# A place of its own for each prologue step on every engine, and two small VectorE operations that read one operand from PSUM

## The chip, the cores and the metric

The kernel runs on one core of one Trainium2 chip. TensorE (PE), VectorE (DVE), ScalarE (ACT), GpSimd (POOL) and SyncE (SP, which only issues DMAs here) each run their own instruction stream in order and meet through semaphores. The metric is the device time in microseconds of one execution.

## What is computed

Eight images (B = 8, 128 channels, 16 x 16 = 256 tokens) go through two residual layers:

```
x = x + L0(groupnorm(x))     # linear attention with rope, a 5x5 depthwise conv of v ("lepe"), a gate o, a projection
x = x + L1(groupnorm(x))     # layernorm, 4 channel groups through a Mamba block, layernorm, a projection

# inside the Mamba block, per channel group and token t (16 states per channel):
delta = softplus(dt @ W_dt.T + b_dt);  A = -exp(A_log)
h = exp(delta_t * A) * h + (delta_t * u_t) * B_t      # a scan over the 256 tokens
y_t = sum over states of h * C_t, then + u_t * D, then * silu(z)
```

## The kernel before

All work is in fp32. The batch index b is the image. The work of an image is split into **chains** of steps, one generator per chain and engine; a step is the code between two `yield`s.

- `front(b)`: normalise, the q, k, v, o products, softmax, rope, and the 128x128 matrix KVM (DVE line 989). In order: xg0, qk, QK and kraw, vo, vpad (its copy goes through DRAM to V4), oS, eff, nmx, exp, rE, kk (line 984, "QK<-F,rE,kraw"), Mk, den, tq and tk on POOL (835, 837), rope, QR and lz, zS, kvT, KVT, kv, KVM.
- `lepe(b)`: eight rounds of conv matmuls on PE (line 404), which need V4 in SBUF.
- `mid(b)`: res on PE, u1 and u2 on DVE (998, 1002), u3 on POOL, proj on PE, sums on ACT, g2 on PE, then ga, nv, ms on DVE (1006, 1009, 1014) with lnv and rs on ACT between nv and ms, xg, xc, sq, var, lr, rr, xl (DVE 1018), XN (ACT 697). XN goes through DRAM (`xn_out`, line 235) and comes back as XN4 in four shifted copies (line 239).
- `tail(b)`: Mamba's inputs. xp, z, dt on PE, the silus, the softplus pieces ab, em, um1, lnu on ACT (714 to 724), cor on DVE (1025), dl1, delta, du on POOL (851 to 858), bc on PE and ACT. bc goes through DRAM and comes back broadcast as Bs and Cs (line 257); delta goes out in the `spill` (246) and comes back broadcast in `load_delta` (265).
- `lead(0)`: the same for image 0 alone; here DVE does dl1 to du (1034 to 1044) and delta is broadcast by PE (line 490, `delta_bc`) instead of through DRAM.
- `weights`: products of weights, and the statistics of images 1 to 7.
- `back(b)`: y2 on DVE (1052), output projection, second layernorm (xl2, 1055), store.

The scan itself is no chain: each image has eight **units** g = 0 to 7. On DVE a unit is one multiply into BIN (line 1082, in PSUM, by Bs) and one scan (line 1107, needs `decay` of ACT, line 789); on POOL it is one multiply by Cs (line 882, `hc`), on PE one `collect` (557), one unit behind. A unit has four slots (segments) in which `side()` runs the steps of other images' chains whose number has come. On DVE two slots lie between multiply and scan and two behind the scan; on POOL two lie ahead of its multiply and two behind.

So the order on each engine is fixed by numbers alone. A **period** of 32 segments holds the eight units of image b and beside them back(b-1), tail(b+1), mid(b+2), front(b+3) and lepe(b+3): the `yield`s are their segments, and on every engine a step with a lower number goes first. What runs ahead of period 1 is a **prologue**: `PROLOGUE` gives each chain of images 0 to 3 an offset and a rate (`at + number * rate // 8`), the same on all engines; START is the segment where image 0's units begin; whatever has a number beyond START + 32 runs behind the units and ahead of period 1. These numbers order instructions on an engine, nothing more: between engines only semaphores count.

```
            for g in range(GROUPS):
                seg = iter(range(START + SIDES * g, START + SIDES * (g + 1)))
                unit(0, 0, g, lambda: segment(works, next(seg)), True)
            run(works, START + SEGMENTS, 7 * SEGMENTS)
            with eng.Fori(0, (B - 4) // 2) as pair:
                period(2 * pair + 1, 1)
                period(2 * pair + 2, 0)
```

The last two images (6, 7) have their units cut in halves (lines 1078, 1094, 1097).

## Time and profile before

| | |
|---|---|
| runs shown | 387.08, 385.05, 385.3 us; median 385.3 |
| profiled execution | 385.47 us, of which the span from the first to the last instruction is 383.7 us |
| mean granted TensorE clock in the span | 0.860 |
| busy, share of span | PE 279.8 us (73%), DVE 282.9 (74%), ACT 221.0 (58%), POOL 201.1 (52%) |
| first multiply of image 0's units | 86.79 us |
| first multiply of period 1 | 128.69 us |
| first multiply of period 6 (half units) | 314.35 us |

Times are microseconds from the span's start. The share of busy time is a mean over stages: ahead of 86.8 us DVE is nearly idle, between 128 and 375 us it is the engine that is busiest.

### The profile page before, as it was taken

How to read it: one execution, taken by the hardware profiler on the slowest of the kernel's cores; microseconds unless marked ns; L12 is line 12 of the kernel's file. 1: busy time of each engine (PE TensorE's matmuls, PEld its weight loads, DVE VectorE, ACT ScalarE, POOL GpSimd, SP SyncE). 2: the span in 40 equal slices, each digit the busy share in tenths (PEclk: the TensorE clock that was granted, in tenths of full speed). 3: DMA queues.
4: the chain of work that ended last, by engine and by line, in shares of the span. 5: the costliest groups of instructions: out<-in, count | busy, mean ns of one | idle time of the engine just before them, and what ended most of it. 6: DMA issues, size and time to landing. Idle time of an engine off the chain costs nothing.

```text
span 383.7 us, 5569 instructions
## 1 busy us (share of the span) xinstructions
PE 279.8 (73%) x1882; PEld 133.0 (35%) x1882; DVE 282.9 (74%) x342; ACT 221.0 (58%) x408; POOL 201.1 (52%) x135
## 2 busy tenths in 40 slices
PE   2398697389849687978796859877986756856764
PEld 1164334153315333433343325334532422312221
DVE  1622242109887699988997799889999989899992
ACT  2324574546845686669765866687657538634211
POOL 0020100014676368746864658458748757967760
PEclk9999699558967988999899878997999669678588
DMA  7230308750048915791589057915890397177000
GB/s 268 73 78 25 86 15 288 290 118 2 30 121 261 331 49 129 262 335 58 126 274 346 33 126 249 332 71 127 277 340 15 93 289 290 41 284 276 2 0 27
DMA packets 27075, 61.73 MB, mean 161 GB/s; under 512 B 2992, under 2 KB 14896, under 8 KB 27056
## 3 DMA queue, kind: packets, MB, share of 16 engines
q1 hardware_dynamic: 26768, 60.88, 49.6%
q10 hardware_dynamic: 288, 0.61, 0.4%
q8 instruction: 11, 0.18, 0.2%
q14 instruction: 8, 0.07, 0.1%
HBM read 54.62 MB, written 6.86 MB: 160 GB/s over the span
## 4 chain that ended last, share of the span: by engine, by line
PE 40%; DVE 21%; ACT 16%; issue 11%; DMA 9%; POOL 1%; SPq 1%; ACTq 0%; DVEq 0%; POOLq 0%
DVE hst L1107 7%; PE F L404 6%; PE DB L530 4%; DMA delta_scratch<-delta 4%; DVE DB L1082 4%; DMA dlt<-delta_scratch 3%; PE Y L557 3%; PE F L382 3%; DVE hst L1094 2%; DVE DB L1078 2%; PE F L373 2%; DVE hst L1097 2%; PE F L352 2%; PE F L390 2%; DMA CCs<-cc 1%
## 5 line engine op out<-in xcount | busy, mean ns | idle before, releaser
L882 POOL TENSOR_TENSOR hst<-hst,Cs 128x1024 f32<-128x1024 f32 x48 | 113.2, 2359 | 62.0 <-DVE hst L1107 62.0
L1107 DVE TENSOR_TENSOR_SCAN hst<-dec,DB 128x1024 f32<-128x1024 f32 x48 | 109.6, 2283 | 1.3
L789 ACT ACTIVATE dec<-dlt,negA 128x1020 f32<-128x1020 f32 x60 | 68.3, 1145 | 21.1 <-DMA dlt<-delta_scratch 14.6
L1082 DVE TENSOR_TENSOR DB<-DB,Bs 128x1024 f32<-128x1024 f32 x48 | 58.9, 1226 | 2.7 <-PE DB L530 1.7
L557 PE MATMUL Y<-hst,CCs 128*32 128x256 f32 x512 | 47.9, 431 | 10.0 <-POOL hst L879 5.4
L879 POOL TENSOR_TENSOR hst<-hst,Cs 128x512 f32<-128x512 f32 x31 | 38.7, 1269 | 15.2 <-DVE hst L1094 15.2
L404 PE MATMUL F<-V,wpatch 128*32 128x256 f32 x512 | 38.4, 419 | 0.9 <-DVE xl L1018 0.9
L846 POOL TENSOR_TENSOR u<-u,oS 128x256 f32<-128x256 f32 x8 | 5.8, 729 | 51.0 <-DVE u L1002 51.0
L835 POOL TENSOR_TENSOR tq<-QK,W0s 128x512 f32<-128x512 f32 x8 | 8.7, 1091 | 42.8 <-DVE QK L984 42.8
L530 PE MATMUL DB<-du,CCs 32*128 32x512 f32 x64 | 22.8, 793 | 8.8 <-DVE DB L1078 5.5
L557 PEld LDWEIGHTS Y<-hst,CCs 128*32 128x32 f32 x512 | 14.9, 117 | 37.0 <-issue 18.1
L404 PEld LDWEIGHTS F<-V,wpatch 128*32 128x32 f32 x512 | 15.2, 117 | 19.1 <-issue 12.9
L989 DVE TENSOR_TENSOR KVM<-F,CCs 128x128 f32<-128x128 f32 x8 | 2.3, 292 | 26.4 <-PE F L390 26.4
L429 PE MATMUL F<-xg,CCs 128*128 128x256 f32 x16 | 8.3, 613 | 17.9 <-ACT xg L682 17.9
L1078 DVE TENSOR_TENSOR DB<-DB,Bs 128x512 f32<-128x512 f32 x32 | 20.5, 687 | 0.6 <-PE DB L530 0.4
L1094 DVE TENSOR_TENSOR_SCAN hst<-dec,DB 128x512 f32<-128x512 f32 x16 | 19.3, 1209 | 0.0
L1097 DVE TENSOR_TENSOR_SCAN hst<-dec,DB 128x512 f32<-128x512 f32 x16 | 19.1, 1194 | 0.0
L773 ACT ACTIVATE X<-F,bout 128x256 f32 (+1 forms) x7 | 3.3, 475 | 26.2 <-PE F L520 26.2
L453 PE MATMUL F<-XN,W1s 128*32 128x256 f32 x112 | 8.4, 421 | 10.9 <-ACT xs L704 10.9
L352 PE MATMUL F<-xg,W0s 128*128 128x256 f32 x32 | 9.8, 434 | 5.0 <-ACT xg L617 4.1
L461 PE MATMUL F<-xs,W1s 128*64 128x512 f32 x14 | 8.2, 668 | 6.9 <-DVE cor L1025 6.9
L622 ACT ACTIVATE r_qk<-F,W0s 128x256 f32<-128x256 f32 x16 | 6.7, 471 | 11.0 <-PE F L352 11.0
(176 smaller groups left out, 538.8 us busy)
## 6 DMA issues: line engine op xcount, KB each, us to landing
Bs<-bc_scratch SPq DMA_DIRECT2D x32, 512.0 KB, 6.5
Cs<-bc_scratch SPq DMA_DIRECT2D x32, 512.0 KB, 7.3
dlt<-delta_scratch SPq DMA_DIRECT2D x15, 512.0 KB, 4.7
V<-v_scratch SPq DMA_DIRECT2D x32, 200.0 KB, 3.7
XN<-xn_scratch SPq DMA_DIRECT2D x28, 128.0 KB, 3.3
delta_scratch<-delta SPq DMA_DIRECT2D x16, 128.0 KB, 4.4
v_scratch<-vpad SPq DMA_DIRECT2D x8, 211.5 KB, 2.1
bc_scratch<-bc SPq DMA_DIRECT2D x8, 128.0 KB
```

The source lines that it names most:

```text
L352: last = mm(F0[:, T * i:T * i + T], wt("wqkvo", C * i, C), xg0[:], start=True, stop=True)
L404: last = mm(F1[CM * q:CM * q + CM, 0:T], wpatch[:, ROUNDS * q + n, :], img[:, :, 0:W], start=(n == 0), stop=(n == ROUNDS - 1))
L530: last = mm(DU[:, half, :], wt("pick")[p0:p0 + DD], du[j][p0:p0 + DD, :], start=True, stop=True)
L557: last = mm(Y[CM * i:CM * i + CM, T * kg:T * kg + T], wt("place"), hst[g % 4][:, T * i:T * i + T], start=False, stop=(g % 4 == 3))
L789: af(dec[g % 4][:, :, 1:T], dlt[2 * j + g // SG][:, :, 1:T], ACT.Exp, scale=negA[:, g:g + 1]).then_inc(S("decay_ready"), 1)
L879: tt(part, part, halves(Cs[g % SG], half), ALU.mult).then_inc(S(signal), 1)
L882: tt(hst[g % 4][:], hst[g % 4][:], Cs[g % SG][:], ALU.mult).then_inc(S("hc_ready"), 1)
L1078: v.tensor_tensor(BIN[:, half, :], DU[:, half, :], halves(Bs[g % SG], half), ALU.mult).then_inc(S(signal), 1)
L1082: v.tensor_tensor(flat(BIN), flat(DU), Bs[g % SG][:], ALU.mult).then_inc(S("b_ready"), 1)
L1094: v.tensor_tensor_scan(halves(hst[g % 4], 0), flat(dec[g % 4][:, 0:2, :]), BIN[:, 0, :], 0.0, ALU.mult, ALU.add).then_inc(S("h_half"), 1)
L1097: v.tensor_tensor_scan(halves(hst[g % 4], 1), flat(dec[g % 4][:, 2:4, :]), BIN[:, 1, :], 0.0, ALU.mult, ALU.add).then_inc(S("h_ready"), 1)
L1107: v.tensor_tensor_scan(hst[g % 4][:], flat(dec[g % 4][:]), flat(BIN), 0.0, ALU.mult, ALU.add).then_inc(S("h_ready"), 1)
```

## The change

Four things, in one diff.

1. `PROLOGUE` goes. Each engine gets a table `places` with one number for each step of each chain, and `segment` takes the step with the lowest number first. START is 100. In the new order image 0's chains come first, then image 1's; the units of image 0 begin on DVE behind lead(0), front(1), u1 and u2 of mid(1) and QK and kraw of front(2).
2. What stood ahead of START and no longer does goes into the 32 segments of image 0's units or, above 132, behind them and ahead of period 1. On DVE ga(2), nv(2), ms(2), cor(1), nmx(3), xl(2), rE(3), kk(3), KVM(3) stand behind the units.
3. The `yield` numbers of the periods 1 to 7 change on all engines. On DVE: u1, u2 and QK 7, 7, 4 to 5, 6, 6; y2 3 to 2; nv and ms from 14 to 15 and 16 (ga stays at 14); nmx 16 to 15; kk 21 to 17; xl2 27 to 24; KVM 31 to 26. On PE: qk 2 to 0, xp 3 to 2, kvT and kv 27 and 29 to 22 and 23, the conv rounds 24 to 30 become 20 to 31. On ACT: lr2 and rr2 27 to 25, KVT 29 to 25, QR and lz 27 to 22, XN 19 to 24, bc 15 to 11. On POOL: u3 2 to 8, delta 13 to 11, tq and tk 19 and 21 to 14. The SP numbers are in the diff.
4. nv and ms read the group mean from F1 in PSUM in place of its copy ga in SBUF.

```diff
-        def begin(chain, b, j, at=0, rate=8):
-
-            steps = chain(b, j)
-            return [steps, at + next(steps, IDLE) * rate // 8, at, rate]
+        def advance(work):
+
+            step = next(work[0], IDLE)
+            work[1] = step if work[2] is None else next(work[2], IDLE)
+
+        def begin(chain, b, j, places=None):
+
+            work = [chain(b, j), 0, None if places is None else iter(places)]
+            advance(work)
+            return work
 
         def segment(works, s):
 
-            for work in works:
-                while work[1] == s:
-                    work[1] = work[2] + next(work[0], IDLE) * work[3] // 8
-
-        def periods(eng, chains, start, unit, finish):
+            while works:
+                work = min(works, key=lambda candidate: candidate[1])
+                if work[1] > s + 1 - 1e-6:
+                    return
+                advance(work)
+
+        def periods(eng, chains, places, start, unit, finish):
 
 
...
-            works = [begin(chain, k, k % 2, *at) for chain, k0, starts in zip(
-                (tail, lead, mid, lepe, front, weights), (1, 0, 0, 0, 0, 0), PROLOGUE) for k, at in enumerate(starts, k0)]
+            works = [begin(chain, k, k % 2, steps) for chain in (tail, lead, mid, lepe, front, weights)
+                     for k, steps in places.get(chain.__name__, {}).items()]
...
-        PROLOGUE = (((130, 9),), ((78, 6),), ((61, 6), (96, 6), (134, 6)), ((16, 12), (61, 7), (88, 13), (122, 9)), ((30, 7), (53, 11), (100, 5), (128, 10)), ((36, 5),))
-        START = 127
+        START = 100
...
             def front(b, j):
 
-                yield 5
+                yield 6
                 sp.wait_ge(S("vpad_ready"), b + 1)
                 sp.dma_start(v_dram, vpad[:]).then_inc(S("v_out"), 16)
-                yield 9
+                yield 17
                 sp.wait_ge(S("v_out"), 16 * (b + 1))
...
             def mid(b, j):
 
-                yield 15
+                yield 21
                 if isinstance(b, int) and b == 0:
                     return
                 sp.wait_ge(S("xn_ready"), b + 1)
                 sp.dma_start(xn_dram, XN[j][:]).then_inc(S("xn_out"), 16)
-                yield 25
+                yield 22
...
             def tail(b, j):
 
-                yield 10
+                yield 17
                 sp.wait_ge(S("bc_ready"), b + 1)
                 sp.dma_start(bc_dram[j].rearrange("w s (h n) -> h (w s) n", h=2), bc[:]).then_inc(S("bc_out"), 16)
-                yield 12
+                yield 17
                 spill(b, j)
-                yield 12
+                yield 18
                 load_delta(b, j, 0)
                 load_delta(b, j, 1)
...
+            places = {
+                "tail": {
+                    1: (96.882, 104.059, 111.235,),
+                },
+                "lead": {
+                    0: (39.471, 46.647,),
+                },
+                "mid": {
+                    0: (3.588,),
+                    1: (68.176, 75.353,),
+                    2: (118.412, 124,),
+                },
+                "front": {
+                    0: (10.765, 17.941,),
+                    1: (25.118, 32.294,),
+                    2: (53.824, 61,),
+                    3: (82.529, 89.706,),
+                },
+            }
+            periods(sp, (weights, front, lepe, mid, tail, back, lead), places, lambda: None, unit, lambda: None)
...
             def lepe(b, j):
 
                 for n, (dy, dx) in enumerate(PLACES):
-                    yield (24, 25, 26, 26, 27, 28, 29, 30)[n]
+                    yield (20, 20, 23, 24, 28, 31, 31, 31)[n]
...
             def tail(b, j):
 
-                yield 3
+                yield 2
                 pe.wait_ge(S("xn_shifted"), 16 * DCONV * b)
...
+                "tail": {
+                    1: (122.6, 125, 127.333, 128.222,),
+                },
+                "lead": {
+                    0: (67.073, 71.951, 100.7,),
+                },
...
+                    1: (98.78, 103.5, 104.9, 111.5, 114.5,),
+                    2: (121.8, 127.111, 127.778, 128, 128.444,),
+                },
...
+                    2: (116.429, 117, 117.571, 118.143, 118.714, 119.4, 120.2, 121,),
+                    3: (128.889, 129.111, 129.333, 129.556, 130, 130.222, 130.444, 146.25,),
...
+                    2: (86.585, 102.1, 106.3, 109, 112.5, 113.5, 115.286,),
+                    3: (115.857, 127.556, 128.667, 129.778, 130.667, 130.889, 176.75,),
+                },
...
-                yield 27
+                yield 22
                 act.wait_ge(S("rope_done"), b + 1)
...
-                yield 29
+                yield 25
                 act.wait_ge(S("kvT_done"), b + 1)
                 nc.scalar.copy(flat(KVT[:]), F0[:]).then_inc(S("kvT_ready"), 1)
...
+                yield 19
                 act.wait_ge(S("xc_done"), b + 1)
...
-                yield 19
+                yield 24
                 act.wait_ge(S("xl_ready"), b + 1)
...
-                yield 6
+                yield 9
                 wait(act, "dl1_ready", b)
                 af(lnu[:], F2[:], ACT.Ln, bias=1.0).then_inc(S("lnu_ready"), 1)
-                yield 15
+                yield 11
                 act.wait_ge(S("bc_done"), b + 1)
                 wait(act, "bc_out", 16 * b)
                 nc.scalar.copy(bc[:], F2[0:2 * 2 * DS, :]).then_inc(S("bc_ready"), 1)
...
+                "tail": {
+                    1: (122.095, 122.476, 123.048, 123.238, 123.81, 124.381, 124.571,),
+                },
+                "lead": {
+                    0: (87.5, 95.833, 104.091,),
+                },
...
+                    1: (105, 107.727, 108.636, 109.545, 114.25, 115.25, 116.25, 116.75,),
+                    2: (122.286, 122.857, 123.429, 123.619, 124.19, 124.952, 125.333, 125.714,),
...
+                    1: (37.5, 40.278, 45.833, 48.611, 51.389, 56.944, 65.278, 70.833, 81.944, 84.722, 90.278,),
+                    2: (93.056, 98.611, 100.455, 101.364, 102.273, 103.182, 105.909, 106.818, 111, 113, 114.75,),
+                    3: (115.75, 117.25, 117.75, 122.667, 124, 124.762, 125.143, 125.524, 125.905, 145.5, 176.5,),
...
+            places = {
+                "tail": {
+                    1: (124, 125.333,),
+                },
+                "mid": {
+                    0: (42.5,),
+                    1: (93.5,),
+                    2: (122.667,),
+                },
+                "front": {
+                    0: (8.5, 25.5,),
+                    1: (59.5, 76.5,),
+                    2: (107, 109,),
+                    3: (145.5, 176.5,),
+                },
+            }
+            periods(pool, (weights, front, lepe, mid, tail, back, lead), places, lambda: None, unit, lambda: None)
...
-                yield 14
+                yield 15
                 dve.wait_ge(S("ga_ready"), b + 1)
-                v.scalar_tensor_tensor(out=nv[:], in0=ga[:, 0:1], scalar=ga[:, 0:1], in1=ga[:, 1:2],
+                v.scalar_tensor_tensor(out=nv[:], in0=F1[:, 0:1], scalar=ga[:, 0:1], in1=ga[:, 1:2],
                                        op0=ALU.mult, op1=ALU.subtract).then_inc(S("nv_ready"), 1)
-                yield 14
+                yield 16
                 dve.wait_ge(S("rs_ready"), b + 1)
                 wait(dve, "xg_ready", b)
-                v.scalar_tensor_tensor(out=ms[:], in0=ga[:, 0:1], scalar=-1.0, in1=rs[:],
+                v.scalar_tensor_tensor(out=ms[:], in0=F1[:, 0:1], scalar=-1.0, in1=rs[:],
                                        op0=ALU.mult, op1=ALU.mult).then_inc(S("ms_ready"), 1)
...
+            places = {
+                "tail": {
+                    1: (154.111,),
+                },
+                "lead": {
+                    0: (79.032, 85.484,),
+                },
+                "mid": {
+                    0: (40.323, 43.548, 56.452, 59.677, 62.903, 75.806,),
+                    1: (88.71, 98.387, 109.167, 109.5, 109.833, 117.5,),
+                    2: (126.333, 127.667, 133.444, 140.333, 147.222, 167.889,),
+                },
+                "front": {
+                    0: (1.613, 4.839, 14.516, 20.968, 24.194, 37.097,),
+                    1: (46.774, 53.226, 66.129, 69.355, 72.581, 82.258,),
+                    2: (91.935, 95.161, 108.167, 108.5, 108.833, 116.5,),
+                    3: (119, 127, 161, 174.778, 181.667, 188.556,),
+                },
+                "weights": {
+                    0: (8.065, 11.29, 17.742, 27.419, 30.645, 33.871, 50,),
+                },
+            }
+            periods(dve, (weights, front, lepe, mid, tail, back, lead), places, lambda: None, unit, lambda: None)
```

## Rows read from the trace of the kernel before

**Rows 1.** Groups of DVE instructions 128.7 to 312 us, shapes apart: xcount, busy, mean ns, idle before

```profile
L1014 DVE SCALAR_TENSOR_TENSOR ms<-ga,rs 128x1 f32<-128x1 f32 x5 | 4.9, 983 | 3.0 <-ACT rs L678 3.0
L1025 DVE SCALAR_TENSOR_TENSOR cor<-um,F 128x512 f32<-128x512 f32 x5 | 3.4, 688 | 2.9 <-ACT lnu L724 2.8
L1052 DVE TENSOR_TENSOR y<-Y,zs 128x512 f32<-128x512 f32 x5 | 3.4, 681 | 2.3 <-PE Y L557 2.3
L1009 DVE SCALAR_TENSOR_TENSOR nv<-ga 128x1 f32<-128x1 f32 x5 | 2.9, 581 | 0.2
...
L1055 DVE SCALAR_TENSOR_TENSOR xl<-F,W1s,rr 128x256 f32<-128x256 f32 x5 | 2.4, 484 | 2.7 <-ACT rr L767 2.7
...
L998 DVE TENSOR_TENSOR u<-F,zS 128x256 f32<-128x256 f32 x5 | 2.1, 419 | 1.3 <-PE F L414 1.3
...
L989 DVE TENSOR_TENSOR KVM<-F,CCs 128x128 f32<-128x128 f32 x4 | 1.2, 292 | 3.6 <-PE F L390 3.6
L1006 DVE COPY ga<-F 128x2 f32<-128x2 f32 x5 | 0.7, 133 | 0.0
```

**Rows 2.** The timeline on DVE: start, us, instruction, idle before it and its releaser

```profile
86.79 1.23 DVE L1082 TENSOR_TENSOR DB<-DB,Bs 128x1024 f32<-128x1024 f32 x1 [1.73 <-PE DB L530]
...
120.73 2.29 DVE L1107 TENSOR_TENSOR_SCAN hst<-dec,DB 128x1024 f32<-128x1024 f32 x1
...
128.69 1.23 DVE L1082 TENSOR_TENSOR DB<-DB,Bs 128x1024 f32<-128x1024 f32 x1
...
314.35 1.30 DVE L1078 TENSOR_TENSOR DB<-DB,Bs 128x512 f32<-128x512 f32 x2
```

**Rows 3.** Three source lines over the whole span: duration in ns, min/median/max

```profile
L1009 DVE SCALAR_TENSOR_TENSOR nv<-ga x8: 219/424/1311, 38.8 to 296.1; 128x1 f32<-128x1 f32 x8
...
L1014 DVE SCALAR_TENSOR_TENSOR ms<-ga,rs x8: 159/784/1700, 39.7 to 297.5; 128x1 f32<-128x1 f32 x8
...
L1018 DVE SCALAR_TENSOR_TENSOR xl<-F,W1s,rr x8: 460/475/483, 44.0 to 302.9; 128x256 f32<-128x256 f32 x8
```

**Rows 4.** The timeline around lead(0), all engines

```profile
51.79 0.69 ACT L748 ACTIVATE ab<-F,W1s 128x512 f32<-128x512 f32 x1
...
52.85 0.67 SPq L283 DMA_DIRECT2D bc_scratch<-bc  x1
...
55.96 0.69 DVE L1044 TENSOR_TENSOR du<-delta,xs 128x512 f32<-128x512 f32 x1
...
58.09 0.58 SPq L257 DMA_DIRECT2D Bs<-bc_scratch  x1
```

**Rows 5.** The timeline on POOL in image 0's units

```profile
105.56 1.25 POOL L851 TENSOR_TENSOR dl<-lnu,cor 128x512 f32<-128x512 f32 x1
...
120.69 2.37 POOL L882 TENSOR_TENSOR hst<-hst,Cs 128x1024 f32<-128x1024 f32 x1
123.02 1.09 POOL L837 TENSOR_TENSOR tk<-QK,W0s 128x512 f32<-128x512 f32 x1
```

**Rows 6.** The chain that ended last: start, us, what

```profile
148.51 5.25 DMA delta_scratch<-delta
153.78 4.02 DMA dlt<-delta_scratch
157.88 1.15 ACT dec L789
```

**Rows 7.** The timeline on ACT in period 3

```profile
216.53 0.60 ACT L717 ACTIVATE F<-ab 128x512 f32<-128x512 f32 x1
```

**Rows 8.** The timeline on the DMA queue of SP, end of period 1, and DVE in period 2

```profile
155.13 0.51 SPq L235 DMA_DIRECT2D xn_scratch<-XN  x1
...
160.56 1.73 SPq L239 DMA_DIRECT2D XN<-xn_scratch  x4
162.41 0.52 SPq L257 DMA_DIRECT2D Bs<-bc_scratch  x1
...
169.84 1.22 DVE L1082 TENSOR_TENSOR DB<-DB,Bs 128x1024 f32<-128x1024 f32 x1
```

More of the change, by code:

```diff
@@ L284, in lead @@
                 load_bc(b, j, 0)
-                yield 16
+                yield 26
                 spill(b, j)
@@ L309, in weights @@
                 yield from ()
-            periods(sp, (weights, front, lepe, mid, tail, back, lead), lambda: None, unit, lambda: None)
+            places = {
[18 more added lines that the diff above has]
+            periods(sp, (weights, front, lepe, mid, tail, back, lead), places, lambda: None, unit, lambda: None)
             sp.wait_ge(S("stored"), 16 * B)
@@ L816, in _ @@
             setup()
-            periods(act, (weights, front, lepe, mid, tail, back, lead), start, unit, lambda: None)
+            places = {
[6 more added lines that the diff above has]
+                "mid": {
[3 rows of a table added]
+                },
+                "front": {
[4 rows of a table added]
+                },
+                "weights": {
+                    0: (20.833, 26.389,),
+                },
+            }
+            periods(act, (weights, front, lepe, mid, tail, back, lead), places, start, unit, lambda: None)
         @block.gpsimd
```

160 lines of the change are left out of this document (87 added, 73 removed), and 6 rows, old and new, of the table places.

## The prediction

> **What bounds the kernel now.** I read the waits of DVE, then the groups of its instructions, then its timeline unit by unit, then the chain that ended last and the DMA queue. Between the first multiply of period 1 (128.69) and that of period 6 (314.35) lie five periods in 185.7 us, 37.1 each [rows 2]. In them DVE works or waits for small things: ms for rs 3.0 us, cor for lnu 2.9, y2 for the last collect 2.3, xl2 for rr2 2.7, u1 for res 1.3, KVM for kv 3.6, together 15.8 us [rows 1]. A second loss is hidden in busy time. nv and ms are one element wide; their shortest cases take 0.219 and 0.159 us, but nv goes up to 1.311 and ms to 1.700, while xl, the same kind of instruction with 256 elements and one tensor from PSUM, stays within 0.460 to 0.483 [rows 3]. In the five periods their means are 0.581 and 0.983, so the excess is 5 x (0.581 - 0.219) + 5 x (0.983 - 0.159) = 5.9 us [rows 1, 3]. Both have SBUF operands only, and POOL is in its long multiply then. Without waits and excess the five periods would be 185.7 - 15.8 - 5.9 = 164.0 us, 32.8 each. So DVE sets the periods, and there is up to 21.7 us to win.
>
> Ahead of period 1 it is otherwise: dependent chains set the time. The units of image 0 begin at 86.79, though du(0), which they need, is done at 56.65 [rows 4]; front(2) and mid(1) stand between. The units end with the scan at 120.73 to 123.02, and 5.7 us of gap follow until 128.69 [rows 2].
>
> **The change, part by part.**
>
> *First multiply of image 0.* I wrote out the new order of each engine and followed it. The start of the profile is the same up to QK and kraw of image 0, and XN(0) comes about 1 us sooner, since mid(0) no longer waits behind front(1). Against it, on ACT ab of lead(0) stands behind KVT(1) and xg0(2): ab moves from 51.79 to about 53.6, and du(0) ends near 58.4 instead of 56.65. Behind du DVE has u1, QK, kraw, u2, until 60.5. Bs(0) is issued at the end of the bc round trip, 58.09 - 52.85 = 5.2 us behind its write [rows 4], so at about 57.2, and lands near 61. First multiply 61; the decays need delta_bc and come at 62.3. The first scan ends near 64.9 instead of 90.3: 25.4 us sooner. Work that stood ahead of it is not gone; it is owed below.
>
> *Image 0's units.* Old: 86.79 to 123.02, 36.2 us [rows 2]. New: 8 units at 3.6 us (multiply 1.23, scan 2.29) are 28.8; beside them stand nmx, rE, kk, ga, nv, ms, KVM, xl, QK, u1, kraw, u2, together 4.1 us; waits inside are 2.0 in unit 2 (eff, exp, lnv and rs in a row) and 1.1 for KVM(2). Sum 36.0, last scan at 97.5; I allow 1 us for what I can't see: 98.5.
>
> *The gap.* Here the debt is paid. ACT takes lnv(2) ahead of em, um1, lnu of tail(1), and DVE reaches ga, nv, ms(2) and then cor(1) only behind the last scan. From the last scan to the end of cor: ga 0.13, nv 0.22, lnv and rs 0.6, ms 0.16, then em, um1, xg, lnu at 0.60 [rows 7], cor 0.69 [rows 1], 4.2 us, with hand-offs and the wait for g2(2) 5.9: 104.4. Then POOL, which has dl1, delta, du *ahead of* its multiplies 6 and 7, and tq, tk(3) behind them: 3 x 1.25 + 2 x 2.37 + 2 x 1.09 + hand-offs 0.4 = 11.1 [rows 5]: 115.5. From tk to the next multiply the old trace takes 128.69 - 124.11 = 4.6 us (kvT, KVT, kv, KVM) [rows 2, 5]; in the new order two decays of 1.15 [rows 6] stand on ACT ahead of KVT: 6.9. First multiply of period 1: 122.4. The other branch, delta through DRAM, ends about there too: delta done at 107, spill 5.25, load 4.02, decay 1.15 [rows 6], 117.4. So the gap is 24 us instead of 5.7, and what remains of the 25 us is 128.7 - 122.4 = **6.3 us**. Bounds: each engine's list may hide waits in the gap (least saving 0, the gap 6 us longer); if all my allowances fall away, 9.
>
> *nv and ms from PSUM.* They become what xl is, one tensor from PSUM, and xl never shows the excess [rows 3]. A PSUM source costs nothing that the rows show: ga copies two elements out of PSUM in 0.133 [rows 1]. **5.9 us** in periods 1 to 5 (bounds 0 and 5.9). The Trainium skill speaks against it: "VectorE: DVE Perf Modes", section on the TRN2 errata, gives a fixed 120 cycles for a PSUM source and 58 for SBUF, an estimate of 65 ns for each of 16 instructions, 1.0 us in all; the 0.133 us of ga is no longer than an SBUF instruction of that width, and the trace decides. For the cause the skill ("SBUF — State Buffer", section "Who interferes with whom") has a lock on a read port between POOL and a DVE instruction with two SBUF inputs, held for a whole instruction; the longest case of 1.7 us against POOL's 2.37 fits it.
>
> *The new order in the periods.* nv at 14 or 15 and ms at 16 put nmx and a multiply between them, which hides lnv and rs: 3.0 us. KVM at 26 needs kk at 17: about 10.5 us of DVE work between them, while the chain kk to KVM needs about 9; besides, QR, lr2, rr2 and KVT of ACT now precede the decay that waits for load_delta. So KVM's 3.6 goes, and of xl2's 2.7 most. lnu comes sooner as qk no longer waits for a KVM at 31: of cor's 2.9, 2 go. u1's 1.3 goes. y2's 2.3 stays: xp stands ahead of that collect now. Sum of waits removed 3.0 + 3.6 + 2.0 + 2.0 + 1.3 = 11.9.
> What is late next: the round trip of XN. XN goes at 24 on ACT, behind a decay, QR, lz, zS; xn_out to XN4 took 160.56 - 155.13 = 5.4 us, XN4's four issues 1.8, and only then is Bs of the next image's unit 1 issued (162.41), 7.4 us ahead of its multiply (169.84) [rows 8]. With shorter periods those 7.4 us shrink by about 1.5 to 2 and some of the load shows: I charge 1.0 us a period, 4.8 in all. Net 11.9 - 4.8 = **7.1** (bounds 3.0, the part that is plain, and 13).
>
> *Periods 6 and 7* have no nv, ms or front; one wait for lnu goes: 0.5.
>
> Sum: 6.3 + 5.9 + 7.1 + 0.5 = 19.8. The profiled execution has 385.5 us, 0.2 above the median of 385.3. 385.5 - 19.8 = 365.7; **366 us**.
>
> **Rivals.**
> *The gap eats the prologue's gain.* The gap chain runs over five engines, and every number in it is a least case. If period 1 starts at 128.7 as now: 385.5 - 13.5 = 372. For it: 24 us of pure dependence. Against it: the sum has slack in the eff and DMA branches.
> *The PSUM operand doesn't do it.* The excess stays, if its cause is another: 366 + 6 = 372. Against it: [rows 3].
> *The order gives its gain back.* Only rs's 3.0 us come from it: 370.
> *Slower: XN's round trip becomes the bound.* Each period would be as long as XN to XN4 to Bs. To lose against now, a period must pass 37.1 + 6.3 / 5 = 38.4, from 32.8: XN must be late by 5.6 us more than the slack, where place 24 instead of 19 explains 2 to 3. At 1.5 us beyond that point: 393. For it: Bs waits in the same queue behind XN4 [rows 8]. Against: SP's spill is now ahead of V4's load, so the loads of delta clear sooner.
>
> **How the numbers follow.** Main case 0.57, own range 358 to 370; gap 0.14; order given back 0.10; PSUM 0.06; XN bound 0.07; the rest 0.06 spread near no change. A measurement here can tell about 0.5% from no change. The range leaves out 0.2: from 357, all allowances falling away, to 378, two of the losses together. Faster 0.87, same 0.05, slower 0.08.
>
> **What would show it.** Right: first multiply near 61, last scan of image 0 near 98, period 1 from 122; a hole in DVE of some 24 us between them with POOL busy in it; nv and ms at 0.2 us in all eight images; no wait at KVM; five periods in some 173 us. Wrong: Bs or XN4 as releaser of DVE or PE in each period; a first multiply of period 1 behind 128; nv or ms still at 0.8.

## The result and the profile after

The changed kernel takes 374.5 us (median of 4 runs, 373.62 to 378.18) against 385.6 (4 runs, 385.05 to 387.08). The ratio is 0.9755, 95% interval 0.971 to 0.980: faster by 11.1 us by the medians, by 9.4 us (7.7 to 11.2) by the ratio. The forecast was 19.8 us and a time of 366. The sign is right and the time lies inside the whole range (357 to 378), but outside the main case's own range (358 to 370), and the gain is about half of the one predicted. In the profiled executions 385.47 becomes 374.03, and the span 383.7 becomes 372.2: 11.5 us to be placed.

(Some executions of a kernel are more than 1.5% longer than its fastest: below, medians and ranges are over all executions, ratios and their intervals leave the longer ones out and decide where the two differ, and the profiled executions of three experiments, V4's load alone, no PSUM operands and the gap, are such longer ones, so that their rows show which wait stands where and not what it costs.)

The page of the kernel after, span and busy times of the engines:

```profile
span 372.2 us, 5571 instructions
PE 274.4 (74%) x1882; PEld 128.2 (34%) x1882; DVE 275.2 (74%) x342; ACT 220.1 (59%) x408; POOL 201.5 (54%) x135
```

Its timeline on DVE, the rows that answer to [rows 2], and the end of the prologue:

```profile
60.49 1.23 DVE L1174 TENSOR_TENSOR DB<-DB,Bs 128x1024 f32<-128x1024 f32 x1 [1.08 <-DMA Bs<-bc_scratch]
...
93.88 2.29 DVE L1199 TENSOR_TENSOR_SCAN hst<-dec,DB 128x1024 f32<-128x1024 f32 x1
...
121.01 0.29 DVE L1081 TENSOR_TENSOR KVM<-F,CCs 128x128 f32<-128x128 f32 x1 [13.76 <-PE F L416]
121.44 1.23 DVE L1174 TENSOR_TENSOR DB<-DB,Bs 128x1024 f32<-128x1024 f32 x1
...
302.40 1.30 DVE L1170 TENSOR_TENSOR DB<-DB,Bs 128x512 f32<-128x512 f32 x2
```

The 11.5 us split by these starts and [rows 2]. Up to the first multiply of period 1: 128.69 - 121.44 = 7.25 gained (forecast 6.3). Periods 1 to 5: 185.66 - 180.96 = 4.7 gained (forecast 13.0). The rest of the program: 69.35 before, 69.8 after, 0.45 lost (forecast 0.5 gained). So 8.3 us are missing in the periods and 1 more at the end, and the prologue gave 1 more than forecast.

By the first multiplies of image 0 of each period in the two timelines, periods 1 to 5 took 36.3, 37.7, 39.9, 37.3, 34.5 before and take 36.6, 37.6, 38.0, 37.5, 31.2 now. The first four take 149.7 us instead of 151.1. The fifth, in which no front and no conv are left, is shorter by 3.3 us, more than the 2.6 a period that the forecast came to. So of the 4.7 us only 1.4 come from the four periods in which all chains run.

The groups of DVE instructions of the kernel after in 123 to 305 us (count, busy us, mean ns, idle us before and what ended it), beside [rows 1]:

```profile
L1144 DVE TENSOR_TENSOR y<-Y,zs 128x512 f32<-128x512 f32 x5 | 3.4, 681 | 2.2 <-PE Y L583 2.2
L1117 DVE SCALAR_TENSOR_TENSOR cor<-um,F 128x512 f32<-128x512 f32 x5 | 3.4, 677 | 1.2 <-ACT lnu L778 1.2
L1147 DVE SCALAR_TENSOR_TENSOR xl<-F,W1s,rr 128x256 f32<-128x256 f32 x5 | 2.4, 482 | 13.4 <-ACT rr L821 13.4
L1090 DVE TENSOR_TENSOR u<-F,zS 128x256 f32<-128x256 f32 x5 | 2.1, 415 | 0.0
L1081 DVE TENSOR_TENSOR KVM<-F,CCs 128x128 f32<-128x128 f32 x4 | 1.1, 278 | 0.2
L1101 DVE SCALAR_TENSOR_TENSOR nv<-F,ga 128x1 f32<-128x1 f32 x5 | 1.1, 219 | 0.2
L1106 DVE SCALAR_TENSOR_TENSOR ms<-F,rs 128x1 f32<-128x1 f32 x5 | 0.7, 149 | 0.0
```

Row by row the forecast held: ms no longer waits for rs (3.0 to 0.0), KVM fell from 3.6 to 0.2, u1 from 1.3 to 0.0, cor from 2.9 to 1.2, and nv and ms run in 219 and 149 ns. One row stands against it: xl2 (line 1147) waits 13.4 us for rr2 where it waited 2.7. Most of what the other waits lost stands at this one place now.

What keeps rr2 is read on the other engines, in the time before the DVE wait. Period 2 of the kernel after, the timeline on the DMA queue of SP:

```profile
173.12 0.36 SPq L225 DMA_DIRECT2D v_scratch<-vpad  x1
174.95 0.56 SPq L279 DMA_DIRECT2D bc_scratch<-bc  x1
176.29 1.14 SPq L253 DMA_DIRECT2D delta_scratch<-delta  x2
177.55 3.16 SPq L229 DMA_DIRECT2D V<-v_scratch  x4
```

on PE and ACT, and the wait on DVE, in the same period:

```profile
181.75 1.03 PE L399 MATMUL F<-tq,CCs 128*128 128x256 f32 x4
...
185.19 1.19 PE L430 MATMUL F<-V,wpatch 128*32 128x256 f32 x16 [2.41 <-DMA V<-v_scratch]
186.31 1.22 PE L540 MATMUL F<-sq,CCs 128*128 128x256 f32 x2
...
187.57 0.47 ACT L818 ACTIVATE lr<-F,CCs 128x256 f32<-128x256 f32 x1 [3.16 <-PE F L540]
188.07 0.42 ACT L821 ACTIVATE rr<-lr 128x256 f32<-128x256 f32 x1
...
188.53 0.48 DVE L1147 SCALAR_TENSOR_TENSOR xl<-F,W1s,rr 128x256 f32<-128x256 f32 x1 [2.85 <-ACT rr L821]
```

Read it upwards. DVE waits 2.85 us for rr2. rr2 and lr2 of ACT wait 3.16 us for the matmul of the variance (line 540). That matmul needed its square at 180.5 (ACT's sq2 ran there), but on PE it stands behind two conv rounds (line 430), which wait 2.41 us for V4. V4's load starts at 177.55, though its own input v_out was written from 173.12 on: on SP it now stands behind the bc write and the spill of delta. The waits of PE over all periods of the kernel after (us in total, times, longest) say that it is so each time:

```profile
PE F L430 <- DMA V<-v_scratch: 10.6, 4, 2.9
```

Two ends moved against each other. V4's load went from place 9 to 17 on SP: it is issued 19.5 us after the period's first multiply (177.55 - 158.08), before at 181.93 - 164.95 = 17.0. The first conv rounds went from places 24 and 25 on PE to 20: they are ready to run some 25 us into the period, before at 194.32 - 164.95 = 29.4. So the first conv round came 12.4 us behind the issue of the load; now PE is ready for it some 5 us behind, and V4 lands 7.6 us behind (185.19 - 177.55).

### The profile page after: what moved, and what is told of

Same layout as the page of the kernel before. It is cut to its first block, busy times and chain, and to the rows that moved or that the text cites. A ratio compares the mean times of both kernels' runs of the same rounds, so it can differ in the third digit from the quotient of the medians.

```text
span 372.2 us, 5571 instructions
## 1 busy us (share of the span) xinstructions
PE 274.4 (74%) x1882; PEld 128.2 (34%) x1882; DVE 275.2 (74%) x342; ACT 220.1 (59%) x408; POOL 201.5 (54%) x135
## 4 chain that ended last, share of the span: by engine, by line
PE 26%; DVE 17%; issue 17%; DMA 12%; ACT 12%; POOL 10%; SPq 4%; POOLq 1%; DVEq 0%; ACTq 0%
POOL hst L958 6%; DVE hst L1199 4%; DMA V<-v_scratch 4%; PE F L430 4%; PE Y L583 3%; DVE DB L1174 3%; DVE hst L1186 2%; PE DB L556 2%; DMA Cs<-bc_scratch 2%; DVE DB L1170 2%; SPq L229 2%; PE F L378 2%; PE F L408 2%; DMA CCs<-cc 1%; POOL delta L931 1%
## 5 line engine op out<-in xcount | busy, mean ns | idle before, releaser
L583 PE MATMUL Y<-hst,CCs 128*32 128x256 f32 x512 | 50.1, 429 | 11.7 <-POOL hst L955 9.5
L430 PE MATMUL F<-V,wpatch 128*32 128x256 f32 x512 | 38.2, 423 | 12.6 <-DMA V<-v_scratch 10.6
L556 PE MATMUL DB<-du,CCs 32*128 32x512 f32 x64 | 21.2, 742 | 4.4 <-DVE DB L1170 3.3
L1147 DVE SCALAR_TENSOR_TENSOR xl<-F,W1s,rr 128x256 f32<-128x256 f32 x8 | 3.8, 480 | 16.4 <-ACT rr L821 16.4
L676 ACT ACTIVATE r_qk<-F,W0s 128x256 f32<-128x256 f32 x16 | 6.7, 470 | 14.4 <-PE F L378 14.4
L408 PE MATMUL F<-CCs,tk 128*128 128x128 f32 x64 | 13.7, 356 | 0.8 <-ACT lz L708 0.8
L408 PEld LDWEIGHTS F<-CCs,tk 128*128 128x128 f32 x64 | 12.7, 267 | 4.3 <-ACT lz L708 2.0
L573 PE MATMUL Y<-xs,dsel 128*32 128x256 f32 x128 | 12.0, 452 | 2.2 <-DVE y L1144 2.0
```

Source lines behind the costliest of these rows:

```text
L408: mm(F0[:, P * blk:P * blk + P], tk[:, which, P * blk:P * blk + P], wt(turn), start=(which == 0), stop=(which == 1))
L430: last = mm(F1[CM * q:CM * q + CM, 0:T], wpatch[:, ROUNDS * q + n, :], img[:, :, 0:W], start=(n == 0), stop=(n == ROUNDS - 1))
L556: last = mm(DU[:, half, :], wt("pick")[p0:p0 + DD], du[j][p0:p0 + DD, :], start=True, stop=True)
L583: last = mm(Y[CM * i:CM * i + CM, T * kg:T * kg + T], wt("place"), hst[g % 4][:, T * i:T * i + T], start=False, stop=(g % 4 == 3))
```

## The experiments

Kernels of one job shared the chip and the runs of the kernel before: its median was 385.8 us (11 runs) for the first job, 385.6 (16) for the second, 384.9 (11) for the third. The executions of one kernel spread by 4 to 12 us, so differences of 2 us between two medians are not relied on. Where us are given "by the ratio", they are the ratio and its interval times the median of the kernel before.

### First job: is it V4's load, and what is PSUM worth?

**V4's load back in front of bc and spill**, on the changed kernel:

```
-                yield 17
+                yield 10
                 sp.wait_ge(S("v_out"), 16 * (b + 1))
```

> One number is changed against the changed kernel: SP issues V4's load at place 10 of a period, ahead of the writes of bc and delta, as before, in place of 17 behind them. Theory A (V4's load comes late because SP stands at the wait for delta; the first two conv rounds then hold PE, var2 behind them, lr2 and rr2 on ACT, xl2 on DVE): the wait of DVE at xl2, 13.4 us in periods 1 to 4, falls under 2 us, PE no longer waits for V4 (10.6 us now), and the time falls by 8 to 12 us, to 363 to 367. Rival B (xl2 is late because ACT has lr2 and rr2 behind QR, lz, zS and XN at places 22 and 24): the wait at xl2 stays above 2 us in each period and the time stays within 2 us of 374.5. Rival C (another engine takes over): xl2's wait goes, but waits for PE or for Bs take its place and the time falls by less than 5 us.

Measured: 371.6 us (368.14 to 375.09), ratio 0.957 [0.952, 0.963], by the ratio 16.6 us below the kernel before (14.4 to 18.7). The waits of DVE and of PE in this kernel, 120 to 302 us:

```profile
DVE y L1144 <- PE Y L583: 14.3, 4, 4.7
```

```profile
PE F L472 <- DMA XN<-xn_scratch: 11.7, 4, 4.0
```

The wait at xl2 is gone, so V4's load was its cause. But nearly the same 14 us now stand at y2, which waits for a collect matmul, which stands on PE behind xp (line 472), which waits for XN4. That is the first link of the rival named in the prediction, XN's round trip; in the changed kernel PE waits nothing for XN4. Against the change the net gain is 2.9 us by the medians and 7.1 by the ratios (4 to 10), and none in the profiled execution, of 374.4 us. That execution has one more loss, which none of the waits above names: its first four periods take 144.5 us against 149.7 in the changed kernel, its fifth 38.2 against 31.2, and in the fifth the granted clock of TensorE is 0.74 against 0.94. More on this at the third job.

**The other remedy: the variance's matmul ahead of the conv rounds**, V4 as late as in the change:

```
-                yield 22
+                yield 20
                 pe.wait_ge(S("sq2_ready"), b + 1)
```

> V4's load stays late, but var2 is issued on PE at place 20, ahead of the two conv rounds that wait for it (22 before). Theory A: the wait at xl2 goes almost wholly, as var2 no longer stands behind the wait for V4; but kvT, KVT and kv still do, so part comes back as a wait at KVM of about 2 us a period; the time falls by 3 to 7 us, to 367 to 371. Rival B: nothing changes, 374.5 within 2.

Measured: 370.3 us (368.61 to 373.83), ratio 0.961 [0.956, 0.966], 15.1 us by the ratio, 4 to 6 below the change. DVE's waits, 120 to 310 us:

```profile
DVE KVM L1081 <- PE F L416: 9.7, 4, 3.4
```

xl2's wait is gone here too, which shows the link through PE's order. V4 is still late (PE waits 8.7 us for it), and what now stands behind the conv rounds is the kv matmul.

**The PSUM operands alone**, on the kernel before: `in0=ga[:, 0:1]` becomes `in0=F1[:, 0:1]` in nv and ms.

> The kernel before with nv and ms reading the mean from F1 in PSUM and nothing else. Theory A (a VectorE instruction of two SBUF tensors waits for GpSimd's running multiply, and DVE sets the periods): nv and ms fall to 0.22 and 0.16 us in all images and the time falls by 5 to 7.6 us, to 378 to 380.5. Rival: the short instructions are cured but the time is given back at the next wait (KVM, cor): under 2 us gained.

Measured: 382.5 us (378.76 to 384.7), ratio 0.985 [0.979, 0.990]: 3.3 us by the medians, 6.0 by the ratio (3.7 to 8.2). Durations of the two lines (min/median/max ns):

```profile
L1009 DVE SCALAR_TENSOR_TENSOR nv<-F,ga x8: 219/219/220, 39.0 to 293.2; 128x1 f32<-128x1 f32 x8
```

```profile
L1014 DVE SCALAR_TENSOR_TENSOR ms<-F,rs x8: 157/158/159, 39.8 to 294.0; 128x1 f32<-128x1 f32 x8
```

The excess goes entirely, as forecast. Whether the time follows entirely isn't decided: the interval of the ratio holds the 5.9 us forecast, while the one profiled execution is only 2.4 us shorter. In it the five periods take 184.2 us instead of 185.7 (period 1 starts 2.1 sooner), and xl2's wait is 6.4 us instead of 2.7, so in this execution most of what the periods should have won came back there.

**The change without the PSUM operands**: the same edit the other way round.

> The changed kernel with nv and ms reading SBUF again. Theory A: their durations go up again to a mean of 0.6 and 0.9 us in periods 1 to 5. Since DVE waits 3.4 us at xl2 behind them in each of periods 1 to 4 in any case, most of that is swallowed by that wait: the time rises by less than 3 us over 374.5. Rival: the whole 5.9 us come back, 380.

Measured: 374.7 us (369.0 to 377.93), ratio 0.963 [0.956, 0.970]: no loss; by the ratio it is even the faster of the two, in another job. nv goes up to 1079 ns and ms to 2347, 10.0 us more in the five periods than in the changed kernel, but xl2's wait is 4.9 instead of 13.4 us, and the five periods take 181.7 us against 181.0. In the kernel as changed no gain of the PSUM operand can be measured: most of what DVE saves by it, it waits at xl2.

### Second job: down the list of limits, and the parts

**xp behind the collect**: the first experiment, and on PE xp at place 3 instead of 2.

```
-                yield 2
+                yield 3
                 pe.wait_ge(S("xn_shifted"), 16 * DCONV * b)
```

> V4's load at 10 and, beside it, xp of the next image at place 3 on PE (behind the last collect, as before) in place of 2 (ahead of it). The run with V4's load early alone moved the wait of DVE from xl2 to y2 (14.7 us in five periods), because PE stood at xp for XN4 with the last collect behind it. Theory A2 (XN's round trip through DRAM is what is late, and it costs only through the collect behind xp): y2's wait falls under 3 us, the time falls by 7 to 11 us against the run with V4 early alone, to 361 to 365. Rival (xp itself is then late, and with it silu, dt, lnu and cor): DVE waits at cor for 2 us and more a period instead, the time stays near 370.

Measured: 369.4 us (365.85 to 371.3), ratio 0.960 [0.954, 0.966], by the ratios no gain over the first experiment; expected were 7 to 11 us. The waits of DVE, 120 to 302 us:

```profile
DVE DB L1174 <- DMA Bs<-bc_scratch: 9.1, 7, 1.8
```

y2's wait is gone as expected, and its place is taken by Bs, which is issued in SP's queue behind XN4.

**XN's write ahead of delta's loads**: the first experiment, and on SP xn_out at 18 instead of 21, load_delta at 19 instead of 18.

> V4's load at 10 and, beside it, SP issues XN's write ahead of the loads of delta (18 and 19) in place of behind them (21 and 18); xp stays ahead of the collect. Theory A2: XN's write no longer queues behind 1 MB of delta, XN4 lands 2 to 4 us sooner, PE's wait at xp (11.7 us in four periods) falls to under 5 and y2's wait with it; the time falls by 4 to 8 us to 364 to 368. Rival (the round trip is bound by its own latency, or SP by XN being late): the wait at xp stays above 8 us.

Measured: 382.0 us (378.76 to 384.94, 12 runs), ratio 0.992 [0.988, 0.996]: 10 us slower than the first experiment by the medians, 13 by the ratios, where a gain was expected. The DMA issues of this kernel (count, KB each, median us from issue to landing):

```profile
Bs<-bc_scratch SPq DMA_DIRECT2D x32, 512.0 KB, 7.7
...
XN<-xn_scratch SPq DMA_DIRECT2D x28, 128.0 KB, 7.2
...
xn_scratch<-XN SPq DMA_DIRECT2D x7, 129.5 KB, 2.3
```

and of the first experiment:

```profile
Bs<-bc_scratch SPq DMA_DIRECT2D x32, 512.0 KB, 6.2
...
XN<-xn_scratch SPq DMA_DIRECT2D x28, 128.0 KB, 3.6
...
xn_scratch<-XN SPq DMA_DIRECT2D x7, 129.5 KB, 4.9
```

The write does land sooner, 2.3 us instead of 4.9. But delta's loads then run beside the XN4 loads instead of beside the write, and these take 7.2 us instead of 3.6. Bs and Cs of the next unit, 1 MB, come closer too: in period 2 delta, Bs and Cs, 2 MB in all, are issued in the 3.0 us ahead of XN4 here (184.42 to 187.42) and in the 7.0 us ahead of it in the first experiment (180.43 to 187.39). Which of the two slows XN4, no run told apart. PE's wait at xp is 16.6 us (from 11.7), y2's 18.2 (from 14.3). Write and loads together take 9.5 us instead of 8.5 by these medians, and Bs behind them 7.7 instead of 6.2.

**The prologue alone**: explicit places and START = 100, but the old yields inside the periods and SBUF operands.

```
-            works = [begin(chain, k, k % 2, *at) for chain, k0, starts in zip(
+            works = [begin(chain, k, k % 2, steps) for chain in (tail, lead, mid, lepe, front, weights)
...
-        START = 127
+        START = 100
```

> The new places of the prologue and START = 100, with the place numbers of the periods, and the SBUF operands of nv and ms, of the kernel before. Theory A: the first multiply of period 1 comes at 121 to 123 as in the changed kernel (128.7 before), and the rest takes the 255 us that it took before: 377 to 380. Rival (the periods' gain in the changed kernel hangs on both together): above 383 or below 375.

Measured: 377.4 us (374.57 to 383.69), ratio 0.979 [0.971, 0.986], 8.2 us by the medians; period 1 starts at 118.86, and the five periods take 184.2 us. This is most of what the whole change gives; the spans of the two profiled executions, 372.8 and 372.2 us, are nearly the same. With the old order in the periods, period 1 starts 2.6 us sooner than in the changed kernel.

**The gap of the changed kernel**: on PE den, rope and kvT of image 3 ahead of the conv rounds, on ACT zS and KVT ahead of the two decays.

```
-                    3: (128.889, 129.111, 129.333, 129.556, 130, 130.222, 130.444, 146.25,),
+                    3: (128.889, 129.3, 129.5, 150, 150.2, 150.4, 150.6, 150.8,),
...
-                    3: (115.857, 127.556, 128.667, 129.778, 130.667, 130.889, 176.75,),
+                    3: (115.857, 127.556, 128.667, 129.1, 129.2, 129.4, 145,),
...
-                    3: (115.75, 117.25, 117.75, 122.667, 124, 124.762, 125.143, 125.524, 125.905, 145.5, 176.5,),
+                    3: (115.75, 117.25, 117.75, 122.667, 124, 124.762, 125.143, 125.524, 125.905, 125.92, 125.94,),
```

> The changed kernel with another order in the gap ahead of period 1: on PE den, rope and kvT of image 3 stand ahead of conv rounds 1 to 7 (rounds 3 to 7 behind kv), and on ACT zS and KVT ahead of the first two decays of period 1. In the changed kernel tq is done at 110.0 but rope starts at 115.45, behind six conv rounds. Theory G (in the gap PE's order, not POOL's chain, ends last): the first multiply of period 1 comes 2 to 4 us sooner, at 117.5 to 119.5, part of which y2 or u2 gives back; the time falls by 1 to 3 us. Rival (POOL's chain or the loads of delta end last): no change at the first multiply.

Measured: 373.5 us (370.65 to 378.86), ratio 0.970 [0.964, 0.976]. Period 1 starts 3.9 us sooner, at 117.50, and then takes 39.7 us instead of 36.6. DVE's waits of this kernel in period 1, where the kernel after has only the one at xl2, 3.4 us:

```profile
DVE y L1144 <- PE Y L583: 3.1, 1, 3.1
DVE xl L1147 <- ACT rr L821: 2.8, 1, 2.8
```

The order in the gap did set the first multiply. What was won is paid back at y2, behind PE's wait of 1.9 us for XN4 at xp: the transfers did not come sooner with the units. (This is read from one execution, of 378.9 us; the last kernel of the third job gives its earlier start back too, at other rows.)

### Third job: the periods alone, and the last limit

**The new order in the periods alone**: old prologue, new yields, SBUF operands.

> The opposite half of the prologue run: the old order of the prologue, with the new place numbers of the periods, nv and ms from SBUF. Theory A (V4's late load at xl2 gives back what the new numbers win): periods 1 to 5 take 182 to 187 us (185.7 before) and the time stays within 2 us of 385.5. With the prologue alone at about -8 and the PSUM operand alone at about -3 the three parts then add up to the change's -11. Rival (the new numbers win by themselves and the prologue loses it): 380 or less.

Measured: 380.9 us (379.94 to 385.42), ratio 0.9925 [0.987, 0.998], 4.0 us by the medians, 2.9 by the ratio (0.7 to 5.0). The periods take 181.6 us; KVM, rs and u1 no longer wait inside them, xl2 waits 5.3. Between what the two theories expected: the order is worth something, and less than the 7.1 us forecast for it.

**Half of delta's load behind Bs**: the kernel with V4 early and xp at 3, and in `tail` on SP the second half of delta's load at place 30.

```
                 load_delta(b, j, 0)
+                yield 30
                 load_delta(b, j, 1)
...
-                    1: (96.882, 104.059, 111.235,),
+                    1: (96.882, 104.059, 111.235, 130,),
```

> V4's load at 10, xp at 3, and the load of delta's second half (0.5 MB, first needed by unit 4 of the next period) at place 30 in place of 18. With V4 early and xp behind the collect DVE waited for Bs 9.1 us. Theory D (what is left late is the DMA traffic in the second half of a period: 1 MB of delta, XN and 1 MB for each unit's Bs and Cs): the wait for Bs falls under 4 us and the time by 2 to 5 us, to 364 to 367. Rival (Bs is late because it is issued behind XN4 on SP, whatever is ahead in the queues): Bs waits stay above 7 us, the time stays at 369.

Measured: 363.9 us (360.25 to 365.88), ratio 0.942 [0.936, 0.947]: 21 us faster than before by the medians and 22 by the ratio, 11 to 13 faster than the change. DVE's waits, 120 to 302 us:

```profile
DVE DB L1175 <- DMA Bs<-bc_scratch: 3.6, 4, 1.1
DVE ga L1099 <- PE F L452: 2.1, 1, 2.1
DVE xl L1111 <- ACT rr L747: 1.4, 1, 1.4
DVE cor L1118 <- ACT lnu L779: 0.6, 2, 0.4
```

Bs's 9.1 us fell to 3.6, xp's wait on PE from 9.5 to 4.0, and periods 1 to 5, 119.65 to 289.14, take 169.5 us, 33.9 each. The prediction had computed 32.8 for a period without waits or excess. That Bs's wait fell under 4 us is what theory D expected and its rival did not. But two things left the way of XN and Bs at once: the traffic of half of delta, and 1.3 us of SP's time for issuing it (in period 2 delta's issues ahead of XN's write take 0.56 us instead of 1.87; from that write to XN4 it is then 4.15 us instead of 5.05). No run separates them.

The five periods are not alike. The first four take 33.3 us on average; the fifth, which has the least work in it, takes 36.2. The rows of the fifth period in the kernel after and in this one (start to end, its length, then busy time and count of PE, PEld, DVE, ACT and POOL; then the granted clock of TensorE, DMA share, GB/s):

```profile
271.17:302.40 31.23, 22.21 (x168) 8.47 (x160) 30.54 (x25) 22.66 (x35) 23.24 (x13) 0.94 0.53 180
```

```profile
252.92:289.14 36.22, 26.03 (x156) 10.19 (x152) 30.84 (x25) 21.80 (x36) 23.32 (x13) 0.77 0.60 199
```

DVE does the same work in both, and PE is busy 3.8 us longer, with fewer matmuls. From 266.9 to 274.9 us the granted clock of this kernel is 0.50, the lower of its two levels (1.2 GHz of 2.4), after 4 us (262.9 to 266.9) in which PE had been busy for 1.4. The same two groups of matmuls in the kernel after, at full clock, and here:

```profile
283.44 1.07 PE L487 MATMUL F<-xs,W1s 128*64 128x512 f32 x2 [0.54 <-DVE cor L1117]
...
285.01 1.13 PE L556 MATMUL DB<-du,CCs 32*128 32x512 f32 x4
```

```profile
266.74 1.97 PE L488 MATMUL F<-xs,W1s 128*64 128x512 f32 x2 [1.01 <-DVE cor L1118]
...
269.64 2.08 PE L557 MATMUL DB<-du,CCs 32*128 32x512 f32 x4
```

The matmul for ga stands behind these, which is the wait of 2.1 us at ga in the list above. In the other kernels with V4's load early and PSUM operands the fifth period is as slow: 38.2, 36.8, 37.7 and 38.3 us at 0.74, 0.78, 0.77 and 0.74. With V4 late and the variance's matmul moved instead it takes 31.9 us at 0.93. So they are 5 to 7 us longer than the changed kernel there; no run was made to take this back, or to show what brings the clock down.

**V4 early and xp at 3, with SBUF operands**, to price the PSUM operand where DVE sets the pace:

> V4's load at 10 and xp at 3, but nv and ms from SBUF. In the changed kernel the waits at xl2 swallowed their excess. Theory A says that here less is swallowed, as the xl2 wait is gone, but the Bs wait behind it still takes a part: the time rises by 2 to 5 us over 369.4. Rival: nothing, 369.4 within 1.5.

Measured: 376.6 us (369.54 to 381.89), ratio 0.964 [0.957, 0.972], against 369.4 and a ratio of 0.960 [0.954, 0.966] with PSUM operands in another job. The medians are 7 us apart, but the ratios only 1.8, which is well inside their intervals, and the profiled executions 3.4 (372.85 and 369.47), of which 3.1 us lie ahead of period 1. So neither the 2 to 5 us expected nor the rival, nothing, is ruled out. The two traces show both sides of it: with SBUF operands the first four periods take 145.3 us instead of 139.8, and the fifth, at a granted clock of 0.89 instead of 0.78, takes 32.5 instead of 36.8. Durations in this kernel:

```profile
L1101 DVE SCALAR_TENSOR_TENSOR nv<-ga x8: 219/1002/1302, 37.9 to 285.5; 128x1 f32<-128x1 f32 x8
```

```profile
L1106 DVE SCALAR_TENSOR_TENSOR ms<-ga,rs x8: 158/686/2341, 38.9 to 286.8; 128x1 f32<-128x1 f32 x8
```

**All together with another order in the gap**:

```
-                    3: (128.889, 129.111, 129.333, 129.556, 130, 130.222, 130.444, 146.25,),
+                    3: (128.889, 129.2, 129.3, 129.6, 129.65, 129.8, 150, 150.2,),
...
-                    3: (115.857, 127.556, 128.667, 129.778, 130.667, 130.889, 176.75,),
+                    3: (115.857, 127.556, 128.667, 129.1, 129.4, 129.7, 145,),
```

> V4's load at 10, xp at 3, delta's second half late, and in the gap ahead of period 1 den, rope and kvT of image 3 ahead of most conv rounds, rounds 1 to 5 in the pauses and 6 and 7 behind kv, KVT ahead of the first decays. Theory D and G together: the first multiply of period 1 comes at 116 to 118.5, two thirds of these 3 us are kept: 2 us less than without the gap's edit, 362 to 365. Rival (period 1 gives the gap's gain back whole, as its tail then waits for XN4 and Bs): the same time as without it.

Measured: 364.0 us (359.72 to 366.96), ratio 0.944 [0.938, 0.949], the same as without it. Period 1 starts at 116.51 instead of 119.65, 3.1 sooner; it takes 33.5 us instead of 32.3 and period 2 takes 35.6 instead of 33.6, which gives it all back. The rows of the waits place it: in period 1 DVE waits 0.8 us for cor and before for nothing, in period 2 it waits 1.9 for Bs and 0.9 for cor instead of 0.9 for Bs alone. Over the whole stretch Bs's waits are 6.3 us instead of 3.6, cor's 5.7 instead of 3.7 (119 to 312 us in both).

## Why the prediction was half right

**First multiply of image 0**: forecast 61, measured 60.49. Right, with its releaser, the Bs load.

**Image 0's units**: forecast last scan 98.5, which is its end, as the gap is counted from there; measured 96.2 (93.88 and 2.29): 2.3 us too late. The length is right, 36.0 forecast and 35.7 measured, though with less work (DVE is busy 31.5 us instead of 32.9) and more waiting (4.2 instead of 3.1). The rest is the start, 0.5 us sooner, the reserve of 1 us, and a slip: 61 and 36.0 make 97.0, and the prediction wrote 97.5.

**The gap**: forecast 24 us from last scan to first multiply, measured 121.44 - 96.2 = 25.3. The size is right; half of the reasoning is not. Its first half ran as written: cor ends at 100.3, 4.1 us behind the scan (forecast 5.9), then POOL works without a pause to tk, which ends at 111.0, 10.7 us (forecast 11.1). After tk I put 6.9 us, and it took 10.4. Rope's matmuls (line 399) were ready when tq and tk were, and started only at 115.45 on PE, behind six conv rounds and the matmul of den. The gap experiment moved these and brought the first multiply 3.9 us forward. So the 6.3 us forecast for the prologue came near the 7.25 measured partly by luck: the units ended 2.3 us sooner, cor and POOL's stretch took 2.2 us less, and the stretch behind tk took 3.5 more.

**nv and ms from PSUM**: the remedy works in all 16 instructions (217 to 219 and 147 to 159 ns; before up to 1311 and 1700 [rows 3]). The size, 5.9 us, holds for DVE's busy time in the five periods, where the two lines lost 6.0. In elapsed time it is 3.3 us by the medians and 6.0 by the ratio alone on the old kernel, nothing that can be measured in the changed one, and undecided with V4 early. I added it to other terms as if nothing stood behind it.

What the excess is, the traces show more closely than the prediction said. In period 3 of the kernel before, on DVE and on POOL:

```profile
222.51 1.01 DVE L1009 SCALAR_TENSOR_TENSOR nv<-ga 128x1 f32<-128x1 f32 x1
224.11 1.70 DVE L1014 SCALAR_TENSOR_TENSOR ms<-ga,rs 128x1 f32<-128x1 f32 x1 [0.60 <-ACT rs L678]
```

```profile
222.23 1.27 POOL L858 TENSOR_TENSOR du<-delta,xs 128x512 f32<-128x512 f32 x1 [0.16 <-POOL delta L855]
223.46 2.34 POOL L882 TENSOR_TENSOR hst<-hst,Cs 128x1024 f32<-128x1024 f32 x1
```

nv ends at 223.52 and du at 223.50; ms ends at 225.81 and POOL's multiply at 225.80. So it is in every case: of the 80 instances in the five kernels with SBUF operands 55 are longer than the shortest, and each of them ends 0.01 to 0.03 us behind the end of a POOL instruction, whichever it is (dl, delta, du, tq, tk or the multiply by Cs). The excess is what was left of POOL's instruction, and not of its long multiply alone, as the prediction had it. In the nine kernels with one PSUM operand none took more than 0.220 us, though in the changed one 9 of the 16 lie wholly inside an instruction of POOL. The Trainium skill's port lock between POOL and a DVE instruction with two SBUF inputs ("SBUF — State Buffer", section "Who interferes with whom") agrees with this. The fixed price of a PSUM source in "VectorE: DVE Perf Modes" of the Trainium skill, section on the TRN2 errata, an estimate of 65 ns from its cycles, isn't seen: nv's shortest case is 219 ns from SBUF alone and 217 with the PSUM operand, ms's 141 and 147.

**The new order in the periods**: here the prediction failed. The failed step is the sentence "of xl2's 2.7 most" would go, and with it the cost of nothing for V4's load, which I saw moved behind the spill and used only as an argument against the XN rival ("SP's spill is now ahead of V4's load, so the loads of delta clear sooner"). I never followed V4 to its reader. What the runs showed in its place: V4 2.5 us later, the conv rounds over 4 us earlier, the variance's matmul behind them, xl2 waiting 13.4 us. Moving either end (V4's load, or the matmul) removes that wait. Where this term has 7.1 us less of waiting, DVE's waits in these periods grew by 2.7 us; part of that is what nv and ms no longer use. Alone on the old kernel the order won 2.9 to 4.0 us. The other removals of the list, 9.9 us, all came or nearly came (rs 3.0, KVM 3.4, cor 1.7, u1 1.3, 9.4 in all), and the 1.0 us a period charged for XN's round trip (which the prediction sums to 4.8, where five periods make 5.0) doesn't show: it appears only where V4 is early. The accounting of DVE from the first multiply of period 1 to that of period 6: before it was busy 167.2 of 185.7 us, after 159.8 of 181.0. So it is busy 7.4 us less and idle 2.7 more (18.5 and 21.1), which makes the 4.7.

**Periods 6 and 7**: forecast 0.5 gained, measured 0.45 lost; within what one execution can tell.

**The rivals.** The gap did not eat the gain. "The PSUM operand doesn't do it" is false as a mechanism; in elapsed time it holds for the changed kernel and, by the interval of the ratio, not for the old one. "The order gives its gain back" is the case that came: of 11.9 us little is left, though through a wait that I didn't name. "XN's round trip becomes the bound" is false for this change and true one step later: it is the first limit once V4 is repaired (11.7 us at xp), and Bs behind it the second. My claim that the periods can go near 32.8 us is borne out by the kernel with all three places moved (33.9, and 33.3 in the first four), so the headroom was read rightly, and the failure was in believing that this order reaches it. TensorE's clock is in no term of the prediction; between before and after it explains none of what is missing (0.90 before and 0.94 after in these periods), but in the kernels with V4's load early it is low in the one period in which they fall behind the changed kernel.

The parts alone give 8.2 + 3.3 + 4.0 = 15.5 us by the medians and 8.2 + 6.0 + 2.9 = 17.1 by the ratios, together 11.1 and 9.4. The shortfall is beyond the intervals by the ratios (7.7 us, give or take 4.6). That each of them alone still finds some slack at xl2, where the waits are 3.2, 6.4 and 5.3 us, and that they use it up together, fits the 13.4 us of the whole change; it is a reading, and no run tested it.

What stays open: why the earlier start of period 1 is given back. In the gap experiment it stands at y2, in the last kernel at Bs and cor of periods 1 and 2; no run moved what stands behind these. Open too is what lowers the clock in the fifth period of the kernels with V4 early, and how much of their remaining time it is.

## What to carry over

A wait that is removed is won only as far as the next chain behind it allows; so for every moved step, a load above all, follow it to its reader, and check the reader's place as well: a load 8 places later and its reader 4 places sooner each looked harmless. When the waits of an engine fall one by one and the period doesn't, look for the one that rose, and read from it backwards over the queues until something waits for no one. And price freed busy time of an engine by its idle time: where the engine waits for a transfer anyway, it is worth nothing until the transfer is repaired. Last, look at each period by itself: a mean of five hid that the fifth alone was 5 to 7 us longer than in the changed kernel, at a lower granted clock of TensorE.

## What the runs showed of the hardware

Small DVE instructions with SBUF operands only, one element wide, took up to 2.35 us (ms, where its shortest is 0.14): all 55 long ones of 80 ended 0.01 to 0.03 us behind the end of a POOL instruction. One operand from PSUM ended it in every instance, even in nv, which still takes its scalar and its other input from SBUF.

The time of a small transfer changed with what was issued just ahead of it, at the same size: XN's write of 129.5 KB landed in 2.3 us with delta's loads behind it and in 4.9 with them ahead, and its loads of 128 KB in 7.2 us with 2 MB issued in the 3.0 us ahead of them and in 3.6 with the same 2 MB spread over 7.0.

With TensorE's granted clock at 0.50 of full the same four matmuls of 512 columns (line 557, 556 in the kernel after) took 2.08 us instead of 1.13.
